# A decoder layer on one core: earlier weight loads, and expert results summed straight from PSUM

## What is computed

```
weights = _router(x, expert_embeddings)              # top 2 of 8 experts, softmax over them
ones = (weights > 0).astype(weights.dtype)
cap_ones = jnp.where(jnp.cumsum(ones, axis=0) <= expert_capacity, ones, 0.0)   # 512 tokens
caw = weights * cap_ones
vals, idx = jax.lax.top_k(caw.T, expert_capacity)
tokens = x_flat[index].reshape(E, expert_capacity, hidden)
inter = jax.nn.relu(jnp.einsum('ech,eih->eci', tokens, first_linear))
out = jnp.einsum('eci,ehi->ech', inter, second_linear)
out = out * vals[:, :, None]
final = jnp.zeros((n_tokens, hidden), x.dtype).at[index].add(out.reshape(-1, hidden))
...
x = _layernorm(x + ffn(x), axis=-1)
```

## Time and profile before

| | us |
|---|---|
| median of 3 runs (1031.75 to 1034.54) | 1032.01 |
| the profiled execution | 1032.13 |
| its span, from the first to the last recorded event | 1030.1 |
| PE busy | 984.8 |
| DVE busy | 823.0 |
| ACT busy | 725.6 |
| POOL busy | 587.0 |

### The profile page before, as it was taken

How to read it: one execution, slowest core, us unless ns; L and a number is a source line. 1 busy time by engine, 2 the same in 40 slices (tenths; PEclk the granted TensorE clock), 3 DMA queues, 4 the chain that set the end, 5 groups by cost and what they waited for, 6 DMA issues and landing times.

```text
span 1030.1 us, 21649 instructions
## 1 busy us (share of the span) xinstructions
PE 984.8 (96%) x7018; PEld 930.8 (90%) x7018; DVE 823.0 (80%) x2087; ACT 725.6 (70%) x1857; POOL 587.0 (57%) x1069
## 2 busy tenths in 40 slices
PE   8989999999999999999999999999999999996993
PEld 7779999999999999999999999999999999885883
DVE  6867878888888888888888888878887877674784
ACT  6676867777777868776877787867786776454761
POOL 4724465665566656565666556555746373516776
PEclk9999999999999999999999999999999999998998
DMA  7662031112211121113110411041105110385542
GB/s 246 207 152 97 25 108 47 51 46 85 68 51 45 62 92 51 46 35 119 51 45 18 136 51 46 11 143 47 44 6 167 43 45 11 130 309 169 151 148 84
DMA packets 63559, 89.77 MB, mean 87 GB/s; under 512 B 15301, under 2 KB 44537, under 8 KB 63449
## 3 DMA queue, kind: packets, MB, share of 16 engines
q1 hardware_dynamic: 57496, 71.90, 22.5%
q0 software_dynamic: 5952, 16.50, 4.7%
HBM read 49.31 MB, written 39.06 MB: 86 GB/s over the span
## 4 chain that ended last, share of the span: by engine, by line
PE 70%; DVE 7%; ACT 7%; DMA 5%; issue 5%; POOL 4%; SPq 2%; POOLq 0%; DVEq 0%; ACTq 0%
PE ps L625 18%; PE ps L627 18%; PE ps L626 18%; PE ps L654 7%; PE ps L733 2%; DMA bs<-slots,tku 2%; POOL bs L2315 2%; DVE nmx L1839 1%; PE ps L771 1%; PE ps L669 1%; DMA xts<-in_xT 1%; PE ps L671 1%; POOL out L2328 1%; ACT hp L1090 1%; SPq L526 1%
## 5 line engine op out<-in xcount | busy, mean ns | idle before, releaser
L2213 POOL TENSOR_SCALAR prob<-prob,rinv 128x333 f32<-128x333 f32 x256 | 143.6, 572 | 234.1 <-DVE rinv L1848 233.6
L625 PE MATMUL ps<-kv_lo,w_hi 128*128 128x256 f32 (+1 forms) x512 | 155.4, 303 | 1.1 <-DVE kv_lo L1399 1.1
L1246 ACT ACTIVATE oT_hi<-ps 128x256 fp32r<-128x256 f32 x126 | 48.5, 385 | 150.0 <-PE ps L671 150.0
L627 PE MATMUL ps<-kv_hi,w_hi 128*128 128x256 f32 (+1 forms) x512 | 153.1, 299 | 0.0
L626 PE MATMUL ps<-kv_hi,w_lo 128*128 128x256 f32 (+1 forms) x512 | 152.7, 298 | 0.0
L1251 ACT ACTIVATE prob<-ps,nmx 128x333 f32<-128x333 f32 x256 | 135.1, 538 | 7.7 <-DVE nmx L1839 7.7
L1399 DVE TENSOR_TENSOR pT_lo<-ps,pT_hi 128x512 fp32r<-128x512 f32 x254 | 130.9, 549 | 0.9 <-ACT pT_hi L1263 0.3
L1839 DVE TENSOR_REDUCE nmx<-ps 128x2 f32<-128x666 f32 x128 | 108.4, 847 | 8.3 <-PE ps L627 7.0
L654 PE MATMUL ps<-ident,prob 128*128 128x128 f32 (+1 forms) x768 | 105.9, 273 | 1.8 <-POOL prob L2213 1.0
L625 PEld LDWEIGHTS ps<-kv_lo,w_hi 128*128 128x128 f32 x512 | 97.3, 190 | 1.7 <-issue 1.5
L627 PEld LDWEIGHTS ps<-kv_hi,w_hi 128*128 128x128 f32 x512 | 97.0, 190 | 0.0
(11 more groups left out here) (330 smaller groups left out, 3323.4 us busy)
## 6 DMA issues: line engine op xcount, KB each, us to landing
wraw<-in_W SPq DMA_DIRECT2D x14, 512.0 KB, 9.2
vcd_hi<-vst_hi SPq DMA_DIRECT2D x10, 512.0 KB, 3.0
vcd_lo<-vst_lo SPq DMA_DIRECT2D x10, 512.0 KB, 3.8
v_hi<-vcd_hi SPq DMA_DIRECT2D x32, 154.0 KB
v_lo<-vcd_hi SPq DMA_DIRECT2D x32, 154.0 KB
slots<-initr SPq DMA_DIRECT2D x9, 522.0 KB, 9.9
xs<-in_x SPq DMA_DIRECT2D x16, 256.0 KB, 4.3
xts<-in_xT SPq DMA_DIRECT2D x15, 256.0 KB, 4.0
```

Of the source, the lines that this page charges most:

```text
L625: pe.matmul(dst, hi1, lo2, start=first, stop=False, skip_group_check=True)
L627: return pe.matmul(dst, hi1, hi2, start=False, stop=last, skip_group_check=True)
L2213: pool.tensor_scalar(prob[:, h % 2, t, 0:KEYS], prob[:, h % 2, t, 0:KEYS], rinv[:, h % 2, t:t + 1], 1.0, ALU.mult, ALU.mult).then_inc(norm ...
```

## The change

1. The stores that fill `slots` at the start: the own rows get only their last five columns (256 packets of 20 bytes), ahead of the experts' rows; the trash rows are no longer filled.
2. The weight loads move: experts 3 and 7 once the last v products are done, 1 and 5 after the last q products (both in the last batch's body), 2 and 6 after the last k products, 4 after the last output projection. Each expert has a semaphore of its own.
3. The row load of expert e+3 is issued after the sums of expert e have landed; before, that of expert e+4 was issued ahead of the store of the sums of e+1.
4. ACT's scaled copy (`result`) goes. DVE's `sum_of` multiplies, adds the base and writes `yo` in one operation per tile, from PSUM. PE's `outer` waits for these sums (`z_set`) where it waited for the copy (`yo_set`).
5. In the ending, ACT and DVE do more of the last relu before they scale expert 6, and POOL gathers for expert 7 ahead of all scatters of expert 6.

```
@@ constants and start (SP)
+        ew_ld = [*part_ld[4:8], inw_ld, xpr_ld, xT1_ld]
...
+                sp.dma_start(own_rows[:, :, D:ROW], initr[:, 0:NT, D:ROW]).then_inc(init_st, 16)
                 for e in range(E):
                     sp.dma_start(slot_rows[e], initr[:]).then_inc(init_st, 16)
-                sp.dma_start(slots[0:OWN, :].rearrange("(t p) c -> p t c", p=P), initr[:, 0:NT, :]).then_inc(init_st, 16)
-                sp.dma_start(slots[TRASH:TRASH + 4 * P, :].rearrange("(s p) c -> p s c", p=P), initr[:]).then_inc(init_st, 16)
@@ weight and row loads (SP)
+                if at(b, B - 1):
+                    sp.wait_ge(v_mm, 4 * B)
+                    expert_weights(3)
+                    expert_weights(7)
+                    sp.wait_ge(q_mm, 4 * B)
+                    expert_weights(1)
+                    expert_weights(5)
...
             sp.wait_ge(k_mm, 8 * B)
-            sp.wait_ge(q_mm, 4 * B)
-            sp.wait_ge(v_mm, 4 * B)
-            expert_weights(range(1, 3), wr_ld[0])
+            expert_weights(2)
+            expert_weights(6)
...
+            sp.wait_ge(wo_mm, 8 * B)
+            expert_weights(4)
...
             slots_of(2)
-            sp.wait_ge(wo_mm, 8 * B)
-            expert_weights(range(3, 4), wr_ld[1])
-            expert_weights(range(4, E), w1r_ld)
...
-            slots_of(3)
...
-                if e + 4 < E:
-                    slots_of(e + 4)
+                if e + 3 < E:
+                    sp.wait_ge(z_st, PART + 32 * (e + 1))
+                    slots_of(e + 3)
@@ outer (PE)
-                    need(pe, yo_set, 4 * e - 2 + 2 * pair)
+                    need(pe, z_set, 4 * e - 2 + 2 * pair)
@@ results (ACT)
-                if e < E - 2:
-                    result(e, u, (0, 1))
-                    scale(e - 1, (2, 3), e - 1)
-                    result(e, u, (2, 3))
...
+                scale(e - 1, range(ST), e - 1)
@@ sums (DVE)
+            def sum_of(e, s, bank):
+
+                u = e % 2
+                need(dve, z_st, PART + 32 * (e - 1))
+                need(dve, fo_set, 4 * (e - 1))
+                base_of(e, s // 2)
+                return dve.scalar_tensor_tensor(out=yo[u][:, s, :], in0=bank, scalar=wsl[:, e, s:s + 1],
+                                                in1=bs[u][:, s, 0:D], op0=ALU.mult, op1=ALU.add).then_inc(z_set, 1)
...
-                dve.wait_ge(yo_set, 4 * e + 2 * half + 2)
-                base_of(e, half)
-                dve.tensor_tensor(yo[u][:, o, :], yo[u][:, o, :], bs[u][:, o, 0:D], ALU.add).then_inc(z_set, 1)
+                dve.wait_ge(o_mm, 2 * e + half + 1)
+                dve.wait_ge(cols_set, 3 * e + 3)
+                for s in (2 * half, 2 * half + 1):
+                    sum_of(e, s, ps[:, 6 + half, (s % 2) * D:(s % 2 + 1) * D])
@@ ending (POOL)
-            finished(E - 2, (0, 1), T_ORDER)
             gather(E - 1)
-            finished(E - 2, (2, 3), T_ORDER)
+            finished(E - 2, (0, 1, 2), T_ORDER)
             power(E, E - 1, slice(0, 2))
+            finished(E - 2, (3,), T_ORDER)
             power(E + 1, E - 1, slice(2, 4))
```

96 lines of the change are left out of this document (30 added, 66 removed).

## The result

The changed kernel takes 1015.32 us (median of 4, 1013.63 to 1016.52), the kernel before 1032.78 (median of 4) in the same comparison: a ratio of 0.9828, 95% interval 0.9807 to 0.9849. The forecast was 1011.0, its range 1007.5 to 1019.0. The profiled execution took 1013.63 with a span of 1011.6, against 1032.13 and 1030.1. That is some 18 us less, or 1.7%, clear of the scatter; the median lies 4.3 us above the forecast, and the profiled execution is the fastest of the four.

A forecast was written before the change was run, and what follows sets the result against it. PE bounds the kernel except at the start, first expert and expert cycle. Gains of 4.3 (start), 11.5 (first expert), some 2 (cycle) and some 4 (ending order), with 0.4 added for losses, gave 1011.0 us, range 1007.5 to 1019.

The forecast's parts named there:

- Place 1: Start: stores delay batch 2's input rows; PE waits 3.08 us, then runs at half clock; gain 4.3, ends 1.4 and 4.8.
- The share ascribed to the own rows: Start: narrowing the own rows' store to 20-byte packets saves between nothing and half of 2.6 us.
- Place 2: First expert: weight loads hold up expert 0's sums and the first gather; moving them brings expert 1's sums 11.5 us earlier.
- Place 3: Expert-to-expert cycle of sums, store, gather and landing: falls from 13.3 us to PE's own 12.17 us.
- The 1.6 us of the row load under the landing gather: Expert cycle: a row load under the gather is taken to lengthen its landing from 2.02 to 3.66 us.
- The first rival: Expert cycle: gathers stay the bound, since the row load delays their landing; cycle 13.5 us, time 1017.5; chance 0.16.
- ACT's copies: Experts: removing 28 scaled copies of 0.47 us on ACT gives nothing by itself, as ACT wasn't late.
- The cover is 5.6 us: Expert cycle: slack between DVE's sums freeing PSUM and PE's next outer product, so holding the banks costs nothing.
- the sign that the prediction itself named for being wrong: Experts: outer(e+1) showing idle time released by DVE's sums would refute the forecast; no PE idle over 2 us between experts 1 and 6.
- The end: After expert 6: gather of expert 7 starts 19.5 us earlier; final scatters at 1005.5 instead of 1022.66, before the start's gain.
- some 4 from the order at the end: Ending: some 4 us of the gain credited to the new order, with expert 7's gather ahead of expert 6's scatters.
- Slower by PSUM held by DVE: Expert cycle: PSUM stays held by DVE until the gather lands, losing 4 us an expert; time 1035; chance 0.02.

The follow-up runs named there:

- the kernel with the banks: The changed kernel with expert 6's third and fourth outer-product tiles in PSUM banks 0 and 1: 1014.8 us, ratio 0.9815 to before.
- the kernel with the splits: The changed kernel with PSUM banks 0 and 1 for expert 6, its fourth scatter before POOL's power, DVE's second weight split between the sums' halves: 1013.4 us.
- the order alone: The changed kernel with only POOL's fourth scatter of expert 6 moved ahead of the first power of expert 7: 1012.6 us, ratio 0.9832 to before.
- the second profile of the changed kernel: Profile from running the changed kernel once more, nothing edited, beside other follow-up kernels: median 1013.8 us, ratio 0.9840 to before.

## Why the prediction was right, and where it was off

*Place 1* (forecast 4.3, ends 1.4 and 4.8). Measured 4.6 in the profiled pair and 2.7 over the repeated runs, both inside the ends. The mechanism, landing of the input rows and a half clock behind PE's wait, was right. The size was worked out from one profile in which the clock had fallen; the profile with 1.85 us of waiting and no fall shows that this half of the term isn't paid in every run. The rows of before couldn't show it. The share ascribed to the own rows was wrong: it is nothing that the runs can show. That the profiled pair came so near the forecast is in part luck: the profile of before was an execution that paid both halves, and the repeated runs, with 2.7, show that not every one does.

*Place 2* (forecast 11.5). The sums of expert 1 came 12.3 us earlier against the mark. Right in size. But the "11.5 from place 2", worked out under the weight loads, was two things: 8.0 from the weights and 4.3 from the row load of expert 3 that no longer stands ahead of the first sums. The prediction named the second in half a sentence and gave it no price; whoever had moved the weights alone on its word would have gained 8. In the finished kernel the moved weight loads are worth 11.0: 8.0 of waiting and the half clock behind it.

*Place 3* (cycle 13.3 to 12.17). Right: 12.14, sums released by PE. The 1.6 us of the row load under the landing gather, which was "I take it" in the prediction, is shown by the kernel with the old row loads (13.2 and 13.9 against 11.8). The first rival, that the gathers stay the bound, missed because 5 us lie between the row load and the last gather. The margin is thin, though: in the kernel with the banks the second halves of the sums waited 0.6 to 2.9 us for their base rows, and PE kept its pace (12.13 to 12.17 us) only because the sums had that much slack before outer(e+1). (A row load and the four tiles of a gather are the same 534,528 bytes; the prediction's 522 and 533 KB are two ways to count them.)

*ACT's copies* (forecast nothing). Right in the time. "The cover is 5.6 us" was worked out for the middle experts and held there. It doesn't hold for expert 6, whose third tile shares a bank with the first: PE waited 2.14 us for a sum that stood on DVE behind the split of the next expert's weights. This wait is missing from the sum, and it is the sign that the prediction itself named for being wrong: outer with idle time released by the sums on DVE, and PE idle for over 2 us between experts 1 and 6. So the cover of 5.6 us was wrongly carried over to expert 6. The wait cost 0 to 1.2 us at the last sum, depending on the clock, since the base rows landed only just then.

*The end* (forecast final scatters at 1001.2 us after the start's gain is taken off, measured 1004.31). Three terms were too small: the last sum is 0.4 us late, with PE's wait and the half clock behind it; 3.1 us from the last sum to the gather instead of 2.2, of which the store's landing is 2.23, as estimated, and the rest passes before POOL issues; and 1.8 us of a gap that the sum didn't have, below. The credit of "some 4 from the order at the end" is the step that failed: undone, the order costs 0.5 in the expert part and nothing that the repeated runs can show. The prediction followed the gather from its own start, 19.5 us earlier, and let the rest of POOL's queue follow; the queue has the same length in both orders, 14.3 and 14.5 us. The total still came near because the forecast added the ending up item by item on POOL and used the 4 us only to share out the gain. Of the 2.6 us between 1011.0 and the profiled 1013.63 these three make 3.1; the 0.4 added for losses in landings goes the other way. The median of the four executions is another 1.7 us above the profiled one; in the repeated runs the start gave 2.7 and not 4.3, which would account for most of it, but that split isn't shown.

*Slower by PSUM held by DVE* (chance 0.02): no sign of a loss from expert to expert. Even with the first gather 11 us late, PE lost only that delay, once.

## What to carry to other kernels

Ask of each load that shares a queue with a critical store or gather what it delays, and price the loads one by one: here two of them, the weights (8 us alone, 11 undone) and the rows (4.5 to 7 undone), made nearly the whole gain, and the restructured arithmetic none. Where an engine's queue is full from a point to the end, changing the order in it moves the start of one item, and the end only by a wait that goes (0.4 to 1.1 us here); count its items before crediting a reordering. A saving that follows from one profile's half clock should be priced with and without the fall.

## What was unexpected in the hardware

*POOL's descriptors wait for DVE.* An indirect transfer's issue on POOL takes 0.95 us, and up to 1.97 (a scatter up to 2.06) where DVE runs a subtraction of two SBUF operands (1.22 us each) at its start (the one case that got ahead of the split is told above); it goes on when that one instruction ends, also if another follows at once. A subtraction with one operand in PSUM didn't do this (in the kernel with the splits an issue at 966.41, within two such from 965.54 to 966.82, took 0.97). The Trainium skill (SBUF — State Buffer, Who interferes with whom) has such an instruction contend with POOL's reads through an exclusive lock, and infers that the making of descriptors isn't touched by it, since that needs the write side. The runs here differ: these transfers take their row numbers from SBUF, and their issue is held back.

*A gap behind the first transfer of the ending.* In every one of the fourteen profiles POOL stands for 2.02 to 2.08 us between the first and the second indirect transfer behind the powers of expert 6, whichever transfer that is (a gather in the changed kernel, [993.09] above; a scatter in the old ending, 994.20 above, and in the kernel before, at 1011.28). It waits for nothing that the profile shows. It goes with the place in POOL's program and not with the kind of transfer. A gap of the same size (2.00 to 2.02 us) stands in all of them ahead of the first of the last four scatters into `slots` (894.39 in the changed kernel). What it is stays open.

*The same wait, two clocks.* 2.14 us of idle PE inside expert 6 was followed by the half clock in the first profile of the changed kernel (0.50 from 983 to 985 us) and in those with the old weights (0.50 from 995 to 997), the old ending (0.50 from 985 to 987) and the order alone (0.54 from 983 to 985), and by the full clock in the second profile of the changed kernel (1.00 from 983 to 987); 1.85 us at the start by the full clock, 3.08 and 9.63 us by the half.
